# Nodes without incoming edges first: half of each dense stage beside the edge stage ahead of it

## The reference, cut to what matters

```python
x = _layernorm(x + L0(x))   # GIN:  relu((x + agg) @ W1 + b1) @ W2 + b2
x = _layernorm(x + L1(x))   # SAGE: h = mean_agg @ W_l.T + b_l + x @ W_r.T; batch norm; relu; + x
x = _layernorm(x + L2(x))   # GAT twice (4 heads of 256, self loops added), then h @ Wfc + bfc
x = _layernorm(x + L3(x))   # GCN:  sum of dinv[row]*dinv[col]*xw[row] with self loops; batch norm; gelu; + x
```

## Time and profile before

| | |
|---|---|
| median of 3 runs (lowest to highest) | 3916.79 us (3909.58 to 3917.03) |
| profiled execution, its own time | 3912.85 us |
| its span | 3911.1 us, 55988 instructions |
| PE busy (share of the span) | 3419.3 us (87%) |
| DVE busy | 2155.2 us (55%) |
| ACT busy | 1463.1 us (37%) |
| POOL busy | 1452.1 us (37%) |
| mean granted TensorE clock | 0.932 of full speed |
| DMA | 821.41 MB, mean 210 GB/s |

### The profile page before, as it was taken

One profiled execution on the slowest core, in us unless ns is written; L12 is line 12 of the kernel. 1 busy time (PEld: TensorE's weight loads), 2 busy tenths in 40 slices (PEclk: granted clock), 3 DMA queues, 4 the chain that ended last, 5 costly groups with the idle time before them and its releaser, 6 DMA issues. The chain is left out here.

```text
span 3911.1 us, 55988 instructions
## 1 busy us (share of the span) xinstructions
PE 3419.3 (87%) x19416; PEld 2074.1 (53%) x19416; DVE 2155.2 (55%) x3972; ACT 1463.1 (37%) x2580; POOL 1452.1 (37%) x1231
## 2 busy tenths in 40 slices
PE   4669998989969999886999999998859999859964
PEld 3234443545637666664666666666635555315543
DVE  7257775845554444276543443413758888406667
ACT  1323332533324444353332332322534444233357
POOL 2345553225422222253333323212536666343312
PEclk7789999989979999997999999999979999979976
DMA  2667774656659999597978878944957777375558
GB/s 82 201 184 198 196 201 146 201 172 228 227 195 259 279 274 281 180 280 213 256 192 204 204 194 198 200 119 146 280 209 259 262 261 262 123 231 186 174 167 275
DMA packets 624227, 821.41 MB, mean 210 GB/s; under 512 B 378374, under 2 KB 378374, under 8 KB 622032
## 3 DMA queue, kind: packets, MB, share of 16 engines
q1 hardware_dynamic: 556880, 598.37, 50.3%
q0 software_dynamic: 67200, 221.25, 20.1%
HBM read 470.83 MB, written 263.59 MB: 188 GB/s over the span
## 5 line engine op out<-in xcount | busy, mean ns | idle before, releaser
L326 PE MATMUL bank<-w_lo,t_r_hi 128*128 128x344 f16 (+1 forms) x2560 | 838.8, 328 | 0.0
L327 PE MATMUL bank<-w_hi,t_r_hi 128*128 128x344 f16 (+1 forms) x2560 | 838.6, 328 | 0.0
L325 PE MATMUL bank<-w_hi,w_lo 128*128 128x344 f16 (+1 forms) x2240 | 716.7, 320 | 49.8 <-DMA w_lo<-g_row_lo 31.3
L2415 DVE SCALAR_TENSOR_TENSOR t_z<-w_lo,t_z 128x256 f32<-128x256 f32 x320 | 243.5, 819 | 396.4 <-DMA w_lo<-h 393.4
L326 PE MATMUL bank<-w_lo,w_hi 128*128 128x344 f16 (+1 forms) x1280 | 419.6, 328 | 0.0
L327 PE MATMUL bank<-w_hi 128*128 128x344 f16 (+1 forms) x1280 | 419.4, 328 | 0.0
L2389 POOL TENSOR_TENSOR t_row_lo<-t_r,t_row_hi 128x1024 f16<-128x1024 f32 x80 | 174.9, 2187 | 509.8 <-ACT t_row_hi L2436 509.8
L327 PEld LDWEIGHTS bank<-w_hi,t_r_hi 128*128 128x128 f16 x2560 | 250.9, 98 | 168.8 <-issue 0.8
L326 PEld LDWEIGHTS bank<-w_lo,t_r_hi 128*128 128x128 f16 x2560 | 250.9, 98 | 162.5 <-issue 0.6
L325 PE MATMUL bank<-w_hi 128*128 128x344 f16 x960 | 298.3, 311 | 21.8 <-DMA w_hi<-t_row_lo 19.2
L325 PEld LDWEIGHTS bank<-w_hi,w_lo 128*128 128x128 f16 x2240 | 219.3, 98 | 181.7 <-issue 50.8
(11 more groups left out here) (345 smaller groups left out, 6732.2 us busy)
## 6 DMA issues: line engine op xcount, KB each, us to landing
w_lo<-h SPq DMA_DIRECT2D x160, 512.0 KB, 5.7
h<-b_wide SPq DMA_DIRECT2D x80, 516.0 KB, 9.6
h<-w_hi SPq DMA_DIRECT2D x80, 516.0 KB, 2.9
sum_gat<-a_out SPq DMA_DIRECT2D x80, 514.0 KB
l_x<-x SPq DMA_DIRECT2D x40, 1024.0 KB, 9.1
sum<-e_out SPq DMA_DIRECT2D x120, 256.0 KB
g_x<-in_x SPq DMA_DIRECT2D x20, 1024.0 KB, 5.6
x<-g_y SPq DMA_DIRECT2D x20, 1024.0 KB, 5.1
```

Source lines behind the costliest of these rows:

```text
L325: pe.matmul(out, s_lo, m_hi, start=(k == 0), stop=False)
L326: pe.matmul(out, s_hi, m_lo, start=False, stop=False)
L327: mm = pe.matmul(out, s_hi, m_hi, start=False, stop=last)
L2415: ins = v.scalar_tensor_tensor(out=z[u][:, s, cols], in0=hrow[:, s, cols], scalar=z[u][:, s, HC + h:HC + h + 1], in1=z[u][:, s, cols], op0 ...
```

## The change

1. Numbering. After the first layer nodes are renumbered: a node's "place" puts nodes without incoming edges first, in both parts by node number. `setup_stage` computes the places (three small POOL operations, three more PE products, two ACT copies, about a dozen DVE operations on 128x80 tables).
2. The first layer (`gin_stage`) still works in node order and stores `x1` plainly. POOL there scatters a small table by place (`by_place`: node, slot, dinv), four indirect DMAs per group with 12 bytes per row, behind the gathers for the group three ahead. `edge_product_stage` reads it back.
3. From `sage_stage` on, groups are in place order. `x1` is fetched by indirect DMA on POOL (`own_rows`), four per group, in `sage_stage` and in `batch_norm_stage`, where SP loaded it before. In `batch_norm_stage` POOL also looks up the places and dinv of each edge's two ends (80 small indirect DMAs, 4 per group); the 40 lookups in `sage_stage` go.
4. `early = (10000 - 5000) // 1024 * 2 = 8` groups hold only nodes without incoming edges. In `sage_stage` they have no gather of sums, no transposes of sums and no add.
5. Three stages of edges alone are replaced. `gat_middle_early_stage`, `rows_product_early_stage` and `gcn_early_stage` run the 8 early groups' dense work, which needs no edge sums, and between its matmul chains the edge work. `gat_middle_stage`, `gat_stage` and `gcn_stage` then run the other 12 groups, with their code unchanged.
6. In the attention edges the scores are spread by a PE transpose instead of a matmul with the identity; the ring of gathered rows has 4 buffers instead of 6, that of outputs 3 instead of 4, and `lhs`, `masked`, the PSUM banks for sums, score rows and denominators are single instead of double.
7. `output_stage` stores by place: POOL scatters each group with four indirect DMAs of 128 rows, after the next group's norm; the negation for the shift moves from POOL to DVE.

The core of the diff (`steps` deals the edge steps out over the slots of dense work):

```diff
+        self.early = max(nodes - edges, 0) // (2 * GROUP) * 2
+def shared_out(steps, slots):
+    return [range(n * steps // slots, (n + 1) * steps // slots) for n in range(slots)]
+def own_rows(kn, pool, out, g, s, landed):
+    pool.indirect_dma_start(out, None, kn.dram["x1"],
+                            bass.IndirectOffsetOnAxis(ap=kn.node_i[:, g * S + s:g * S + s + 1], axis=0), ...
@@ gin_stage, POOL
+        def store_by_place(k):
+            pool.indirect_dma_start(dram["by_place"], bass.IndirectOffsetOnAxis(ap=kn.place_at_i[:, k:k + 1], axis=0),
+                                    kn.by_place[:, k, :], None, ...
             if g + 3 < G:
                 load_sums(g + 3)
+            for k in range(g * S, g * S + S):
+                store_by_place(k)
+        pool.wait_ge(table_out.sem, table_out.at(16 * d.blocks))
@@ sage_stage, PE
-                turn_sums(g, m)
+                if g >= E:
+                    turn_sums(g, m)
@@ batch_norm_stage, POOL
+        for g in range(G):
+            norm.pool(pool, *divmod(g, 2))
+            if g + 2 < G:
+                load_own(g + 2)
+            bias(*divmod(g, 2))
+            for out, at, t in ends[g * per:(g + 1) * per]:
+                look_up(kn, pool, out, at, t, found)
@@ AttentionEdges (W, O = 4, 3)
+    def matrices(self, dve, t):
+        dve.wait_ge(self.den_done.sem, self.den_done.at(t + 1))
+        v.tensor_tensor(self.out[o][:, A_DEN], self.den_ps, self.weight[u][:, 0, :], ALU.add)...
+        if t + 2 < self.T:
+            self.scores(dve, t + 2)
+        ...reciprocal, leak(t + 2), normalise
+        dve.wait_ge(self.summed.sem, self.summed.at(t))
+        v.scalar_tensor_tensor(out=self.lhs[:], ...
+    def tensor(self, pe, t):
+        pe.wait_ge(self.lhs_ready.sem, self.lhs_ready.at(t + 1))
+        for h in range(HEADS):
+            ins = pe.matmul(self.total[h // 2][:, (h % 2) * C:(h % 2 + 1) * C], self.lhs[:, h, :], ...
+        if t + 1 < self.T:
+            self.sum_weights(pe, t + 1)
+        if t + 2 < self.T:
+            self.score_rows(pe, t + 2)      # 4 x pe.transpose
@@ gat_middle_early_stage, PE (E = 8 groups, N = 32 subtiles)
+    steps = shared_out(edges.steps(), THIRDS * N)      # 45 steps over 96 slots
+        edges.tensor_start(pe)
+        for j in range(N):
+            pe.wait_ge(turned_in[s].sem, turned_in[s].at(g * 32 + 32))
+            for third in range(THIRDS):
+                pe.wait_ge(wide_done.sem, wide_done.at((j - 1) * THIRDS + third + 1))
+                split_product(pe, mm[third], ...)      # 24 matmuls of 344 columns
+                for e in steps[j * THIRDS + third]:
+                    edges.tensor_step(pe, e)
@@ rows_product_early_stage, PE: steps = shared_out(45, E * S = 32)
+                if g + 1 < E:
+                    turn(g + 1, (2 * s, 2 * s + 1))
+                split_product(pe, mm[s % 2][:], ...)   # 24 matmuls of 512 columns
+                for e in steps[g * S + s]:
+                    edges.tensor_step(pe, e)
@@ gcn_early_stage, PE: steps = shared_out(41, 4 * E = 32), the same form, 12 matmuls a slot
@@ output_stage
-            sp.dma_start(node_rows(dram["out"], *divmod(g, 2)), x[g])...
+        def store(g):
+            pool.wait_ge(rows_out.sem, rows_out.at(g * S + S))
+            for s in range(S):
+                pool.indirect_dma_start(dram["out"],
+                                        bass.IndirectOffsetOnAxis(ap=kn.node_i[:, g * S + s:g * S + s + 1], axis=0), ...
```

## The result

| | before | after |
|---|---|---|
| median of 4 runs (lowest to highest) | 3913.18 us (3907.46 to 3917.03) | 3812.53 us (3810.86 to 3817.86) |
| ratio, 95% interval | | 0.9746 (0.9728 to 0.9765) |
| profiled execution, span | 3912.85 us, 3911.1 us | 3817.86 us, 3816.0 us |

The forecast was 3849 us (68 less than before) with a range of 3812 to 3900. The time fell by 101 us by the medians and by 95 us between the two profiled executions: the direction was right, the forecast gain was too small by a third, and the time lies only 0.5 us inside the lower end of the range.

What follows compares the result with a forecast made beforehand. PE was taken to bound nearly all dense stages, while edge stages and output left it partly idle. Terms -44 -15 -29 -11 +7 +1 +3 +20 = -68 us took 3912.85 to 3845, plus 3.94 for the median: 3849 us, range 3812 to 3900.

Steps and rivals of the forecast that it cites:

- the three pairs: First attention with middle stage, second attention with `gat_stage`, edge sums with `gcn_stage`; saving under 60 us would refute the forecast.
- rival D: Early fills overlap edge work (-15), no waits in double slots (-18), output's end hidden (-5): 3811 us; chance 0.13.
- Attention edges (step 2.70 us): PE time per attention tile between dense chains: 2.70 us, so 40 tiles take 108 us, 114 with joins.
- First pair: First attention and middle stage: 1061 us before, early stage 477 with fill 20, late 540: -44 us.
- Second pair: Second attention and `gat_stage`: early stage 365 us, 13 double slots each waiting 1.4 us for `lhs`, fill 25: -15 us.
- Edge sums: Edge sums and `gcn_stage`: 1.02 us of PE per tile, fill 13, early stage 162 us: -29 us.
- `sage_stage`: 8 groups lose 16 transposes each (-13.8), gathers by POOL add 3 at the start: -11 us, bounds -15 to 0.
- First dense stage, setup, batch norm: Late scatters at the first's end +7 us, setup's added operations +1, batch norm's POOL loads and lookups +3.
- Rival C: POOL becomes the bound of the first dense stage, 25.0 us a group against PE's 21.0: +80, 3929 us; chance 0.07.
- Rival B: DMA decides where already full: batch norm +30, output +35, giving 3891 us; chance 0.15.
- Output: Last stage: period 7.1 us a group adds 10, scatters after the last norm add 10: +20 us, bounds +5 to +35.
- Rival A: Steps between chains cost the old loop's 3.85 us a tile, DVE's chain not being ahead: about 3923 us; chance 0.04.

Runs made afterwards that it cites:

- e2: Changed kernel with the scores spread by four float32 matmuls with the identity per tile again, in place of four transposes: 3849.91 us, ratio 0.9832.
- a0: The changed kernel itself, measured a second time: 3820.57 us, ratio 0.9756.
- e8: Changed kernel with the first dense stage's four scatters per group made twice, the second time into a table that nothing reads: 3853.2 us, ratio 0.9844.
- e7: Changed kernel with 3 more lookups of 128 rows per group in the second layer's batch norm stage, into an unread buffer: 3824.02 us, ratio 0.977.
- e5: Changed kernel with each output group stored by one plain SyncE DMA, rows left in place order: 3801.25 us, ratio 0.9708.
- e9: Changed kernel with 4 early groups in place of 8: 3926.32 us, ratio 1.0019.

## Why the prediction was right, and its size too small

The mechanism was the one forecast: the three pairs saved 112 us, where under 60 would have spoken against it. The range held by a narrow margin and partly by luck: its lower end was rival D's 3811 us, rounded, and D's mechanism didn't happen.

- **Attention edges (step 2.70 us): the term that was mis-sized.** It measures 2.33. I took start-to-start times from a loop in which the products follow a wait. 0.37 x 40 = 15 of the 18 us missing in the first pair. In the third pair the same mistake in the edge sums' tile (1.02 for 0.86) gives 0.16 x 41 = 7 of 8. What the transposes are worth is shown by e2: +34 us over 80 tiles, 0.43 each. In its trace four matmuls between chains take 0.97 us from start to start, where the four transposes take 0.47, a factor of two. The factor of four that the Trainium skill states for transpose mode ("TensorE: Matmul & The Clock Gate", *Terms*) is not seen.
- **First pair: right otherwise.** Fill 20 (1624.8 to 1645.05), PE at 100 of 100 us, a late stage shorter by 32 x 10.5 us.
- **Second pair: -12.9 for -15, close by luck.** Errors cancel. The 29 steps behind dense work are cheaper by 0.37 each, 11 us. The waits are 23.9 us for 18: the wait for the single `lhs` is as forecast for each slot (1.4 us), in 9 slots where I counted 13, and 11 us come from the late load of the residual's input, which I had not counted. The fill is 27 for 25. And I left out the clock: 0.93, 0.97 and 0.93 in three windows of 50 us is 50 x (0.07 + 0.03 + 0.07) = 8.5 us, an estimate. These make +6 for the new stage, which is 2 over; 4 us stay open.
- **Edge sums: right,** fill 12.7 for 13.
- **`sage_stage`: -10.6 at first, -3.0 in a0.** In nine profiles of it with 8 early groups it took 285 to 286 us three times and 291 to 294 six times. In a0 PE waits for DVE before the transposes of the sums, 9 times 0.3 us, and is busy 98% in the late groups. What decides between the two is open.
- **First dense stage, setup, batch norm: right.** Rival C (POOL as the bound) is shown by e8 to be real and about 3 us of POOL time a group away: 8 x 1.51 + 5.8 = 17.9 us of 21.0, where I had reckoned 19.3. The Trainium skill ("SBUF — State Buffer", *Who interferes with whom*) has GpSimd and VectorE share a port pair that one of them locks at a time. Such a hold-up of the added issues is not seen: they took 1.04 us on average beside the same DVE work. Why the gathers take 1.38 here and 1.00 in the last dense stage no run shows. Rival B's lookups cost nothing in the steady part (e7).
- **Output: +19.8 for +20,** for partly another reason: 8.6 us come from the longer period (for 10) and 12 from the end (for 10). Of the 8.6 us half stays in e5 and goes with DVE's negation, which I had costed at 0.2 us and then hidden under DMA and POOL.
- **Rival A: wrong with 8 groups, nearly right with 4.** I argued that one chain (3.5 us) covers 2.9 us of DVE work. e9 shows that this was the wrong quantity: with one chain to a step the gathered rows come too late, and the steps are 6.93 us apart.
- **Rival D** gave 3811 us, close to what was measured, but through shorter fills and vanished waits, and neither happened (fills of 20, 27 and 13 us, 23.9 us of waits).

## What to carry to other kernels

Work that is laid between dense matmul chains costs the bound engine its start-to-start time behind dense work, which here was less than the trace of its own loop shows (2.33 for 2.70 us); take that time from a place where no wait precedes it. The loop's own pace doesn't vanish: compare it with the distance between steps before cutting its rings or the number of groups. Here it was 6 us; at a distance of 9.8 us the loop was hidden, at 5.84 it was not, and 6.93 came of it. In a merged stage an engine that works in order also carries the dense work's waits into the loop, as the late load of the residual's input did. An edit on an engine that isn't the bound (the transposes) can be worth nothing before such a merge and a third of the gain after it.

## What the runs showed that I had not expected

Rings of 4 and 3 buffers in place of 6 and 4 cost the attention loop 60% more time (3.85 to 6.1 us a tile), and the granted clock fell from 1.00 to 0.80 with it, which makes the gaps dearer. In the second new stage the dips of the clock belong to three gaps of the eleven. Behind the eight gaps of 0.89 to 1.75 us the product records take 1.99 us; behind those of 6.25, 2.71 and 4.72 us they take 3.78, 3.54 and 3.78, about twice as long, which is what the lower level of the clock would give.
